# Two edge sums of a graph network: one chunk in 56 fetched by SyncE row by row, the rest gathered by GpSimd

## The reference

```
x = x + gnn0(layernorm(x), src, dst, edge_weight)     # sum over edges, a product, batch norm, relu
x = x + ffn0(layernorm(x))                            # top half of the nodes
x = x + gnn1(layernorm(x), src, dst, edge_weight)     # sum over edges, two products, norm
x = x + moe(layernorm(x))                             # 8 experts, 2 a node

# the sum over edges, in gnn0 and in gnn1:
aggr = segment_sum(edge_weight[:, None] * table[src], dst, 6250)
```

## Time and profile before

| | us |
|---|---|
| median of 3 runs (3527.41 to 3529.43) | 3528.44 |
| span of the profiled execution, first to last instruction | 3521.7 |
| first edge sum, first gather to the end of its block | 385.3 to 1383.8 |
| second edge sum, first gather to the end of its block | 1786.2 to 2798.1 |
| PE, DVE, POOL busy over the span | 2647.4, 2613.3, 2208.3 |

### The profile page before, as it was taken

How to read it: one execution, slowest core, us unless ns; L and a number is a source line. 1 busy time by engine, 2 the same in 40 slices (tenths; PEclk the granted TensorE clock), 3 DMA queues, 4 the chain that set the end, 5 groups by cost and what they waited for, 6 DMA issues and landing times. The chain is left out here.

```text
span 3521.7 us, 55765 instructions
## 1 busy us (share of the span) xinstructions
PE 2647.4 (75%) x15311; PEld 2239.6 (64%) x15311; DVE 2613.3 (74%) x6603; ACT 1008.4 (29%) x2073; POOL 2208.3 (63%) x2147
## 2 busy tenths in 40 slices
PE   6888466666666665899967677777776569999998
PEld 4777344454444444789945555555555459999997
DVE  6999566666666666969967777777777778888886
ACT  0011000000000002545511111111111168888886
POOL 0455577777777774345557777777777326666664
PEclk9999687878878787899978888888788779999999
DMA  3011433333333332000133333333333447776775
GB/s 98 10 44 33 120 105 105 105 105 105 105 105 105 105 105 73 1 2 31 37 103 111 113 112 111 113 113 111 113 111 113 133 134 216 213 218 211 219 211 140
DMA packets 164679, 389.01 MB, mean 110 GB/s; under 512 B 46378, under 2 KB 95602, under 8 KB 151019
## 3 DMA queue, kind: packets, MB, share of 16 engines
q0 software_dynamic: 99072, 233.49, 24.4%
q1 hardware_dynamic: 65387, 152.94, 12.8%
HBM read 343.97 MB, written 42.98 MB: 110 GB/s over the span
## 5 line engine op out<-in xcount | busy, mean ns | idle before, releaser
L1081 POOL DMA_INDIRECT g_got<-table,e_source x1568 | 1492.1, 952 | 506.5 <-issue 458.9
L1174 PE MATMUL psum<-g_got,g_route 128*128 x3328 | 1087.2, 485 | 642.0 <-DMA g_got<-table,e_source 253.6
L1174 PEld LDWEIGHTS psum<-g_got,g_route 128*128 128x128 f32 x3328 | 760.9, 239 | 888.4 <-issue 763.5
L1107 DVE TENSOR_TENSOR A<-A,psum 128x256 f32 x1664 | 698.5, 420 | 523.6 <-PE psum L1174 345.1
L1090 DVE TENSOR_SCALAR g_route<-columns,e_local,e_weight 128x128 f32<-128x128 f32 x1664 | 472.5, 363 | 17.7 <-issue 12.9
L368 POOL DMA_INDIRECT records<-rec,place x120 | 148.7, 1239 | 220.6 <-ACT rec L580 122.0
L1582 POOL TENSOR_TENSOR f_ht_lo<-f_ht,f_ht_hi 128x512 fp32r<-128x512 f32 x100 | 133.7, 1341 | 187.8 <-ACT f_ht_hi L1531 182.1
L142 PE MATMUL psum<-e_xt_hi,e_w_hi 128*128 128x256 f32 x832 | 238.0, 286 | 5.5 <-issue 5.3
L142 PE MATMUL psum<-e_w_hi,e_ht_hi 128*128 128x256 f32 x832 | 233.1, 280 | 3.1 <-DVE e_w_lo L1981 3.1
L144 PE MATMUL psum<-e_xt_hi,e_w_lo 128*128 128x256 f32 x832 | 233.8, 281 | 0.0
L143 PE MATMUL psum<-e_xt_lo,e_w_hi 128*128 128x256 f32 x832 | 233.7, 281 | 0.0
(11 more groups left out here) (420 smaller groups left out, 5198.5 us busy)
## 6 DMA issues: line engine op xcount, KB each, us to landing
e_w<-in_m_w SPq DMA_DIRECT2D x104, 1024.0 KB, 5.0
g_got<-table,e_source POOLq DMA_INDIRECT x1568, 2.8
expert_table<-g_normal SPq DMA_DIRECT2D x52, 128.0 KB
table<-xn SPq DMA_DIRECT2D x49, 128.0 KB, 1.7
X<-in_x SPq DMA_DIRECT2D x1, 6144.0 KB
table<-f_ring SPq DMA_DIRECT2D x24, 256.0 KB, 2.1
out<-X SPq DMA_DIRECT2D x1, 6144.0 KB
f_w<-in_f_w SPq DMA_DIRECT2D x2, 1024.0 KB, 7.3
```

The source lines that it names most:

```text
L1081: pool.indirect_dma_start(got[:, c % RING, :], None, rows, bass.IndirectOffsetOnAxis(ap=source[:, c:c + 1].bitcast(U32), axis=0)).then_inc ...
L1107: dve.tensor_tensor(to, to, sums_of(c), ALU.add).then_inc(added, 1)
L1174: ins = pe.matmul(sums_of(c), route[:, c % (GB + GSEM), :], row(got, at[j % GSEM]), start=True, stop=True)
```

## The change

In both sums, chunk 55 of every 56 (`HAND`; 14 of 784) is no longer gathered by GpSimd. SyncE fetches its 128 rows with 128 DMAs of one row each, into three places of their own behind the ring's (`HAND_PLACES`), used in turn. For that SyncE loads the row numbers into `expert`, a row of 128 numbers on one partition, 64 at a time (`ask`), and then eight at a time into registers (`fetch`, `LOAD`). GpSimd skips these chunks; TensorE also waits for their rows. `slot_ring` gets the new places, which adds six VectorE steps to `order_slots`.

In the first sum SyncE fetches the first such chunk ahead of the parameter loads and the other thirteen behind them. In the second it fetches 160 rows, and then, for each tile that it stores, 8 rows between the store's issue and the wait for its landing, and the rest of that step's share behind it: `handed(k)` rows are out after step k, 16 chunks' share a step.

The core of the diff:

```diff
+HAND = RING - 1
+HAND_PLACES = 3
+PLACES = HAND + HAND_PLACES
+ROUND = HAND_PLACES * RING
...
+def place_of(c):
+
+    return HAND + c // RING % HAND_PLACES if c % RING == HAND else c % RING
...
+                    turn_no, hand_no = slot_values[:, 0, :], slot_values[:, 2, :]
+                    count_started(turn_no, RING)
+                    count_started(hand_no, ROUND)
...
+            def ask(self, sp, i, h):
+                c = self.chunks[i]
+                sp.dma_start(self.numbers[:, h, :], kept_fields[0][h * self.HALF:(h + 1) * self.HALF, c:c + 1].rearrange("p a -> a p"),
+                             allow_slow_non_contiguous=True).then_inc(hand_numbers_in, 16)
+
+            def fetch(self, sp, got, rows, pairs_summed, start, end):
+
+                for r in range(start, min(end, P * len(self.chunks)), self.LOAD):
+                    i, p = divmod(r, P)
+                    h, c = p // self.HALF, self.chunks[i]
+                    if r == 0:
+                        self.ask(sp, 0, 0)
+                    if p == 0 and c >= ROUND:
+                        sp.wait_ge(pairs_summed, (c - ROUND + NT - 1) // 2 + 1)
+                    if p % self.HALF == 0:
+                        sp.wait_ge(hand_numbers_in, 16 * (2 * (self.before + i) + h + 1))
+                    _, nodes = nc.values_load_multi_w_load_instructions(
+                        self.numbers[0:1, h, p % self.HALF:p % self.HALF + self.LOAD], engines=(mybir.EngineType.SP,), min_val=0, max_val=NT * P - 1,
+                        skip_runtime_bounds_check_because="a source is a node")
+                    for j in range(self.LOAD):
+                        sp.dma_start(got[p + j:p + j + 1, place_of(c), :], rows[bass.ds(nodes[j], 1), :]).then_inc(hand_landed[(self.before + i) % HAND_PLACES], 16)
+                    if p % self.HALF == 0 and i + h < len(self.chunks):
+                        self.ask(sp, i + h, 1 - h)
+
+            def wait_landed(self, pe, q):
+
+                for i, c in enumerate(self.chunks):
+                    if c // GSEM == q:
+                        pe.wait_ge(hand_landed[(self.before + i) % HAND_PLACES], 16 * P * ((self.before + i) // HAND_PLACES + 1))
...
-                got = here("got", [P, RING, D])
+                got = here("got", [P, PLACES, D])
...
+                        hand.fetch(sp, got, rows, pairs_summed, 0, P)
                         for to, of in ((f0_gamma, g0_gamma), (f0_beta, g0_beta), (f0_bias, g0_bias), (f0_b1, f0_b1_in)):
...
+                        hand.fetch(sp, got, rows, pairs_summed, P, P * CHUNKS)
                         sp.wait_ge(params, 144)
                     if through_mlp:
+                        handed = lambda k: (P * (GB * k + RING + GB)) // RING // hand.LOAD * hand.LOAD
+                        hand.fetch(sp, got, rows, pairs_summed, 0, handed(0))
                         for k in range(FINISHES):
                             tiles_of.store_normal(sp, k, tile_to_finish(k + 1, mybir.EngineType.SP))
+                            hand.fetch(sp, got, rows, pairs_summed, handed(k), handed(k) + hand.LOAD)
+                            tiles_of.let_normal(sp, k)
+                            hand.fetch(sp, got, rows, pairs_summed, handed(k) + hand.LOAD, handed(k + 1))
...
                             for c in range(first, first + GSEM // 2):
+                                if c in hand.chunks:
+                                    continue
                                 pool.indirect_dma_start(
-                                    got[:, c % RING, :], None, rows,
+                                    got[:, place_of(c), :], None, rows,
...
                                 pe.wait_ge(gathered[q % 8], gathered_after(q))
+                                hand.wait_landed(pe, q)
```

More of the change, by code:

```diff
@@ L55 @@
 assert MIN_PAIRS > PEELED and (MTILES - 2 * MIN_PAIRS) * MT % (2 * P) == 0
-assert EP * EJ == E and NG * GC == EJ and RUNS_D * RUN * P < BIG and CHUNKS % GSEM == 0 and SLOTS % GB == 0 and RING % GSEM == 0 and NT % GROUP == 0 and GROUPS % 2 == 1
+assert EP * EJ == E and NG * GC == EJ and RUNS_D * RUN * P < BIG and CHUNKS % GSEM == 0 and CHUNKS % RING == 0 and SLOTS % GB == 0 and RING % GSEM == 0 and NT % GROUP == 0 and GROUPS % 2 == 1
 LN_EPS = 1e-5
@@ L512, in order_slots, with count_started @@
                     s(dve.tensor_tensor(slot_hi, slot_hi, slot_lo, ALU.add))
[L513 to L518, removed]
+                    def count_started(to, every):
+                        n = (CHUNKS - 1) // every
+                        past, start = passed_of[:, :, 0:n], ring_start[:, 0:n]
+                        s(dve.tensor_scalar(start, columns[:, 1:1 + n], float(every), None, ALU.mult))
+                        s(dve.tensor_tensor(past, chunk_of_slot[:].unsqueeze(2).to_broadcast([P, SLOT_COLUMNS, n]),
+                                            start.unsqueeze(1).to_broadcast([P, SLOT_COLUMNS, n]), ALU.is_ge))
+                        s(dve.tensor_reduce(to, past, AX.X, ALU.add))
+                    turn_no, hand_no = slot_values[:, 0, :], slot_values[:, 2, :]
+                    count_started(turn_no, RING)
+                    count_started(hand_no, ROUND)
                     s(dve.tensor_scalar(slot_tile_f, slot_values[:, 1, :], rank_tile_f[:, 0:1], None, ALU.add))
-                    dve.scalar_tensor_tensor(ring_no, ring_no, -float(RING), chunk_of_slot[:], ALU.mult, ALU.add).then_inc(map_ready, 1)
+                    s(dve.scalar_tensor_tensor(hand_no, hand_no, -float(HAND_PLACES), turn_no, ALU.mult, ALU.add))
+                    s(dve.scalar_tensor_tensor(ring_no, turn_no, -float(RING), chunk_of_slot[:], ALU.mult, ALU.add))
+                    s(dve.scalar_tensor_tensor(hand_no, ring_no, float(HAND), hand_no, ALU.is_equal, ALU.mult))
+                    dve.tensor_tensor(ring_no, ring_no, hand_no, ALU.add).then_inc(map_ready, 1)
                     dve.wait_ge(bounds_in, 48)
@@ L961, in store_normal, with let_normal @@
                              self.normal[:].rearrange("p (a d) -> p a d", a=1)).then_inc(self.landed, 16)
+            def let_normal(self, sp, k):
                 sp.wait_ge(self.landed, 16 * k + 16)
@@ L1001, in build, with __init__ @@
         gathered = [sem(f"gathered{u}") for u in range(8)]
+        class HandRows:
+            LOAD = 8
+            HALF = P // 2
+            def __init__(self, turns, before):
+                self.chunks = [RING * k + HAND for k in turns]
+                self.before = before
+                self.numbers = expert[:].rearrange("a (h p) -> a h p", h=2)
+            def ask(self, sp, i, h):
[23 more added lines that the diff above has]
+                        pe.wait_ge(hand_landed[(self.before + i) % HAND_PLACES], 16 * P * ((self.before + i) // HAND_PLACES + 1))
@@ L1003, in aggregate, with gathers_of @@
+        hand_numbers_in, hand_landed = sem("hand_numbers_in"), [sem(f"hand_landed{u}") for u in range(HAND_PLACES)]
+        hands = (HandRows(range(CHUNKS // RING), 0), HandRows(range(CHUNKS // RING), CHUNKS // RING))
+        def gathers_of(q, hand):
+            return [c for c in range(q * GSEM, (q + 1) * GSEM) if c not in hand.chunks]
         def aggregate(rows, name, through_mlp, source, local, weight):
@@ L1009, in aggregate @@
             FINISHES = STEPS - 1
+            hand = hands[through_mlp]
             with ExitStack() as scope, nc.Block() as block:
                 here = lambda what, shape, dt=F32: sb(name + what, shape, dt, scope)
-                got = here("got", [P, RING, D])
+                got = here("got", [P, PLACES, D])
                 route = here("route", [P, GB + GSEM, P])
@@ L1027, in gathered_after @@
                 def gathered_after(q):
-                    earlier = -(-(CHUNKS // GSEM - q % 8) // 8) if through_mlp else 0
-                    return (earlier + q // 8 + 1) * (16 * GSEM)
+                    own = sum(len(gathers_of(at, hand)) for at in range(q % 8, q + 1, 8))
+                    before = sum(len(gathers_of(at, hands[0])) for at in range(q % 8, CHUNKS // GSEM, 8)) if through_mlp else 0
+                    return 16 * (before + own)
                 def sums_of(c):
@@ L1165, in _ @@
                                 pe.wait_ge(gathered[q % 8], gathered_after(q))
+                                hand.wait_landed(pe, q)
                             asked[0] = landed_by(first) + 1
                             _, at = nc.values_load_multi_w_load_instructions(
-                                slot_ring[0:1, first:first + GSEM], engines=(mybir.EngineType.PE,), min_val=0, max_val=RING - 1,
+                                slot_ring[0:1, first:first + GSEM], engines=(mybir.EngineType.PE,), min_val=0, max_val=PLACES - 1,
                                 skip_runtime_bounds_check_because="the ring's places are below its size")
@@ L1790, in build @@
             added = [sem("e_added0"), sem("e_added1")]
-            finished = sem("e_finished")
             QUARTER = HB * MT // 4
```

1 line of the change is left out of this document (added).

## The result

The changed kernel took 3603.11 us (median of 4 runs, 3601.86 to 3605.02) against 3528.18 us before: a ratio of 1.0212, 95% interval 1.0200 to 1.0225. I had forecast 3512, in a range of 3500 to 3590. The profiled execution took 3601.86 us, its span 3600.0.

The account below looks back on a forecast made before the run. GpSimd's gather stream was taken to bound both sums. Gains of 7.3 us in the first and about 9 in the second took 16 us off the 3521.7 span, to 3505.4; the median's 6.7 offset gave 3512, range 3500 to 3590.

Parts of the forecast that it names:

- GpSimd's period and the worth of a gather: Both sums: GpSimd starts a gather every 1.256 us, so 14 fewer are worth 17.6 us a sum.
- the setup's cost hidden under ScalarE's copy: Ordering of slots: six added VectorE steps, 1.3 us, cost nothing because ScalarE's copy covers 2 us.
- the one stall in the first sum: First sum: GpSimd waits once, at its chunk 60, 10.3 us for the late first hand chunk, leaving a 7.3 us gain.
- SyncE would set the pace through the handshake over `normal`: Second sum: SyncE's step of 19.15 us exceeds 18.56, holding VectorE, TensorE and GpSimd; gain about 9 of 17.6 us.
- the slope, one for one, of SyncE's time: Second sum: 10 ns more per row lengthen it by 18 us, since SyncE is the bound.
- SyncE's row is dearer: Rival: row DMA 0.288 us, row 0.527, second sum 60 us later, total 3586; chance 0.24 (slower by SyncE's pace).
- the signs that I had named: Trace: row DMAs 0.25 us, rows near 0.43, one GpSimd gap near 10 us, steps 19.15 us; SyncE stalls would contradict.
- the price of a row on SyncE: Both sums: instructions, DMA, gaps, register load and number DMA total 0.489 us a row, 62.6 us a chunk.
- the limit of 14: Second sum: SyncE's lag above 14 us holds VectorE; it starts 5 us behind and meets this near step 15.
- Later chunks are not late: First sum, after the first hand chunk: SyncE makes one in 62.6 us, and GpSimd gives it 69.1.
- The rule of the Trainium skill: Row DMAs: transfers under 64 KB are mostly overhead, about 2 us each; one behind another, 3584 us a sum.
- the rival of the busy lane: Rows may all use one of 16 DMA engines; far bound 3729 us, lane put at 59%; far above had chance 0.08.

Follow-up runs that it names:

- f7: Changed kernel with only every second turn's chunk brought, from the second turn on (7 a sum): 3508.77 us, ratio 0.9958 to the kernel before.
- f8: Changed kernel with stores issued by ScalarE, 16 registers a load, no hand chunk in a sum's first turn (13 a sum): 3495.21 us, ratio 0.9923.
- f6: Changed kernel with one load of 16 row numbers in place of two of 8: 3563.36 us, ratio 1.0113 to the kernel before.
- e4: Changed kernel without register loads and addresses, rows from fixed (wrong) places of the table: 3524.28 us, ratio 0.9990 to the kernel before.
- e3: Changed kernel with the second sum's stores issued by ScalarE and VectorE itself waiting for their landing: 3517.70 us, ratio 0.9964 to the kernel before.
- e1: Changed kernel with SyncE fetching chunks in the first sum only: 3529.77 us, ratio 1.0007 to the kernel before.
- f5: Changed kernel with two buffers for the normalised tile, so VectorE may be one tile ahead: 3588.40 us, ratio 1.0179 to the kernel before.
- e5: Changed kernel with two buffers for the normalised tile, in the batch where the kernel before took 3928.57 us: ratio 1.2213.
- e8: Changed kernel with ScalarE's stores, 16 registers a load, no first-turn hand chunk, in the batch where the kernel before took 3928.57 us: ratio 1.1893.
- e6: Changed kernel with 16 registers a load instead of 8, in the batch where the kernel before took 3928.57 us: ratio 1.1986.
- e7: Changed kernel with every second turn's chunk only brought, in the batch where the kernel before took 3928.57 us: ratio 1.0251.

## Why the prediction was wrong

**What held.** GpSimd's period and the worth of a gather (f7, f8); the setup's cost hidden under ScalarE's copy (the last of the new steps starts at 360.83, the copy at 362.28, 361.99 before; the first gather starts 1.15 us later than before, of which 0.74 are one longer gather of records at 372.75, and with one profile of each it isn't shown that any of it is the edit's); the place of the one stall in the first sum; that in the second sum SyncE would set the pace through the handshake over `normal`; and the slope, one for one, of SyncE's time (f6). The result lies close to the rival "SyncE's row is dearer" (3586), though not for its reason: that rival wanted a slower row DMA, and the row DMA turned out faster than in any of my cases. That the rival's number came so near is luck. Of the signs that I had named, the row DMA spoke for the forecast and the steps (20.50 us) and SyncE's gaps against it.

**The step that failed** is the price of a row on SyncE: 0.489 us forecast, 0.534 measured, and in it the register load. Term by term, per row:

| term | forecast | measured |
|---|---|---|
| register operation, move, row DMA, gaps | 0.43 | 0.408, and 0.004 for the longer first DMA behind a load (260 ns) |
| register load with its gap, over 8 rows | 0.046 | (0.781 + 0.03) / 8 = 0.102 |
| number DMA and the longer load behind it, over 64 | 0.0125 | (0.511 + 0.19) / 64 = 0.011 |
| long gaps, one before every 128th instruction (last section) | 0 | 14.5 / 1792 = 0.008 |
| sum | 0.489 | 0.533 |

I had built the eight-register load from two rows that don't carry it: 268 ns for one register on a SyncE that had just waited, and 9 ns for a further register from VectorE. In the changed kernel a one-register load of SyncE (L1109) takes 0.27 us only behind something other than a DMA, and 0.54 behind a row DMA; a load of eight takes 0.53 behind the store of 128 rows, 0.78 behind a row DMA and 0.97 behind the number DMA. So it is 0.25 us dearer behind a row DMA than in its cheapest place, and from one register to eight (0.54 to 0.78 behind a row) 0.035 us each, not 0.009. These steps make no rule: a load of eight behind the landing wait (L983, itself right behind a DMA) takes 0.72, the next eight registers in f6 cost 0.056 us each behind a row, and behind the store a load of sixteen takes 1.17 where one of eight takes 0.53. I had given every DMA a range and the load none, though it was the one instruction without a row of its kind. An estimate: had it cost 0.33, SyncE would have needed 0.45 x 224 = 101 us less in the second sum: 989, below the 991.8 at which e4 ran at GpSimd's pace, so the full gain would have come there. No run has such a load.

**The second sum.** By my own sum, with the measured prices: 1792 rows at 0.534 instead of 0.489 are 81 us; 45 stores at 1.37 instead of 1.27 are 5; the start of the sum was 1 us later. That puts the end of the rows at 2812, and they ended at 2812.9; the agreement says little, for 1.37 is itself the difference of e3 and this kernel. Two smaller terms: I let VectorE go on with the 47th tile as soon as the 46th had landed and counted that as the time of its store, but that store started at 2822.85, 8.8 us behind the one before it at 2814.07, of which only 2.5 were the landing. And SyncE was late at the very first store, 1879.7 against 1866.7 before, some 13 us, so the limit of 14 was met in the first steps and not near step 15.

**The first sum.** Gain 7.3 forecast, none measured. TensorE's wait for the first hand chunk, and its waits for hand chunks in 400 to 1380 us:

```profile
473.84 2.50 PE L1255 MATMUL psum<-g_got,g_route 128*128 x5 [17.31 <-DMA g_got<-table]
```
```profile
PE psum L1255 <- DMA g_got<-table: 35.2, 6, 17.3
```

The first hand chunk was issued by 471.9 and not 466.6 (5.3 us, the price of the row again). TensorE's group started at 473.84, forecast 468.6; GpSimd's next gather followed it by 2.9 us, where I had allowed 1.1; and the second stall adds 1.7. The 17.6 us of the fewer gathers were spent on one chunk. "Later chunks are not late" was wrong as well: TensorE waited for the next five hand chunks too, 2.0 to 5.8 us each (in e1 for one of them), though only the 1.7 us above reached GpSimd, and it waited for none from the seventh on.

**The rule of the Trainium skill** ("DMA: Bandwidth & Descriptors", "Rules for kernel authors") spoke against the change, and the change did lose; but not by its price. Rows started 0.408 us apart with landings that overlap (the last row of the first chunk was issued at 471.94, and TensorE could start on it 1.9 us later), and f7 and f8 make 1792 and 3328 such transfers of 1 KB and are faster than before.

**The lane.** Nothing in the runs speaks for the rival of the busy lane. The DMA records have 11648 packets more on SyncE's queue than before: two for each of the 3584 rows, one of 1024 bytes and one of 4, and 80 for each of the 56 number DMAs. A row thus goes in one piece, a median of 0.05 us in the second sum, against 0.53 us between rows.

**What stays open.** Why a register load on SyncE is longer behind a DMA isn't settled: the runs show that it is so, and that its time counts in full.

## What to carry to other kernels

An engine that "only issues" has a budget like any other: price every instruction of its loop, register loads first, and measure the one that has no row of its own kind in that place before building on it. Where such a stream also carries a handshake that others wait for, put the two on different engines (e3 turned a loss of 2.1% into a gain of 0.4%) before making the stream cheaper. The first piece of work of a new helper is late by its whole length; leave it to the old path (f7, f8).

## What the runs showed of the hardware that I had not expected

**Every 128th instruction of SyncE stands behind a gap.** SyncE executes 12664 instructions instead of 1386, and q14 brought 212 packets instead of 124. In the two sums 91 gaps of 0.33 to 0.37 us stand ahead of one of SyncE's instructions, 31 us in all, and from each to the next it is exactly 128 instructions, whatever their kind. At the median 1.0 us behind such a gap a packet of 8 KB starts on q14. e3 and f5 to f8 have the same gaps, with a few missing (each time 256 instructions from one to the next). So the gap belongs to the supply of instructions; whether SyncE waits there for instructions or spends the time on asking for the next isn't shown.

**A batch in which a long SyncE program was far dearer.** e5 to e8 ran in a batch in which the kernel before took 3928.57 us (3919.83 to 3936.72), 11% more than in the others. The record gives the same chip number, 14, for it as for f5 to f8, where the kernel before took 3523.36 some seven minutes later; so it isn't shown that the chip made the difference. The ratios were 1.2213 (e5), 1.1986 (e6), 1.0251 (e7) and 1.1893 (e8), where the same kernels had 1.0179, 1.0113, 0.9958 and 0.9923 in the later one. Line 1054 of SyncE in e5, and GpSimd's waits there:

```profile
L1054 SPq FUSED_REGOPS  x3584: 1/37/1408, 411.5 to 4025.2; - x200
L1054 SPq MOVE g_got<-table x3584: 1/29/1468, 411.6 to 4025.2; - x200
L1054 SPq DMA_DIRECT2D g_got<-table x3584: 1/225/1402, 411.7 to 4025.3; - x200
```
```profile
POOL g_got L1161 <- PE psum L1255: 1051.5, 143, 43.4
```

The medians are those of the usual batches (in f5 the longest are 51, 43 and 329 ns), but in over 100 stretches of about 18 instructions each one of SyncE takes 0.7 or 1.4 us, register operations and moves too: some 1500 us in all. GpSimd's gathers keep their length (median 949 ns in e5). Nearly all the extra time lies in the two sums (1622.0 and 1593.6 us in e5, 984.3 and 1071.5 in f5); what follows the last store takes 724.7 us, against 724.8 in f5. The cause is open: the stretches don't come every 128 instructions, as the gaps above do, and where the 400 us of the kernel before went in that batch isn't known, for no trace of it was taken there. All verdicts of this study rest on e1 to e4 and f5 to f8.
